# Copying the first attention's output tiles out of PSUM on another engine, and at another place in its program

## What is computed

```python
x = x + _L0_attn_ref(_layernorm(x), Mq, Mk, Mv)
x = x + _L0_ffn_ref(_layernorm(x), w_gate, w_up, w_down)   # blockwise FP4 rounding of x, weights and hidden values
x = x + _L1_attn_ref(_layernorm(x), w_qkv, ...)            # 16 heads of 16, layer norm of q and k
x = x + _L1_ffn_ref(_layernorm(x), W, b, R, A, B)          # top 2 of 8 low-rank experts
```

```python
scores = jnp.einsum('bhqk,bhck->bhqc', q, k).reshape(B * H, C, C)
att = jax.nn.softmax(scores / jnp.sqrt(jnp.float32(K)), axis=1)
out = jnp.einsum('bqhc,bhcd->bqhd', att.reshape(B, C, H, C), v)
```

## Time and profile before

| | us |
|---|---|
| median of 3 runs | 2735.5 (2731.2 to 2738.0) |
| the profiled execution, its own time | 2732.15 |
| its span, first to last instruction | 2730.4 |
| TensorE busy | 2515.6 (92%) |
| VectorE busy | 2032.0 (74%) |
| ScalarE busy | 1932.9 (71%) |
| GpSimd busy | 1211.5 (44%) |
| mean granted TensorE clock | 0.989 of full speed |

### The profile page before, as it was taken

How to read it: one execution, slowest core, us unless ns; L and a number is a source line. 1 busy time by engine, 2 the same in 40 slices (tenths; PEclk the granted TensorE clock), 3 DMA queues, 4 the chain that set the end, 5 groups by cost and what they waited for, 6 DMA issues and landing times.

```text
span 2730.4 us, 114318 instructions
## 1 busy us (share of the span) xinstructions
PE 2515.6 (92%) x50126; PEld 1391.3 (51%) x50126; DVE 2032.0 (74%) x4228; ACT 1932.9 (71%) x2767; POOL 1211.5 (44%) x1744
## 2 busy tenths in 40 slices
PE   6776877999999999999999999999999999999898
PEld 4445654345744566345654466445663457433434
DVE  6778866967888589866888589875888678875634
ACT  4552456886778767877778867787668777787685
POOL 4564466226743277125752167223772157411300
PEclk9988999999999999999999999999999999999999
DMA  5214332325423353324423343233532253232410
GB/s 133 47 37 82 60 67 75 67 42 96 112 54 82 60 120 79 70 51 85 109 72 77 50 98 92 63 66 59 122 93 53 51 99 91 61 70 41 92 37 25
DMA packets 458137, 200.60 MB, mean 73 GB/s; under 512 B 270110, under 2 KB 447622, under 8 KB 457614
## 3 DMA queue, kind: packets, MB, share of 16 engines
q1 hardware_dynamic: 455982, 192.15, 33.5%
q10 hardware_dynamic: 1632, 0.79, 0.2%
HBM read 46.48 MB, written 32.51 MB: 29 GB/s over the span
## 4 chain that ended last, share of the span: by engine, by line
PE 43%; DVE 22%; ACT 9%; DMA 8%; POOL 6%; issue 6%; SPq 4%; ACTq 0%; DVEq 0%; POOLq 0%
PE pR L765 16%; PE pV L1032 10%; ACT ub L1345 6%; DVE nmaxa L1648 6%; PE pS L989 6%; PE pS L765 5%; PE pV L890 3%; PE pR L775 2%; DMA xT<-ua 2%; DMA ua<-ua 2%; SPq L2655 1%; POOL ua L2182 1%; SPq L716 1%; DMA ua<-EA 1%; DMA xT<-xhb 1%
## 5 line engine op out<-in xcount | busy, mean ns | idle before, releaser
L1345 ACT ACTIVATE ub<-pS 128x1024 f32<-128x1024 f32 x1024 | 988.5, 1023 | 208.3 <-PE pS L989 198.9
L1648 DVE TENSOR_REDUCE nmaxa<-pS 128x1 f32<-128x1024 f32 x512 | 620.8, 1216 | 147.8 <-PE pS L765 145.2
L1281 ACT ACTIVATE ua<-pS,nmaxa 128x1024 f32<-128x1024 f32 x384 | 427.5, 1114 | 248.8 <-DVE nmaxa L1648 244.7
L765 PE MATMUL pS<-ua 128*32 128x512 f16 x8192 | 540.9, 384 | 59.9 <-ACT ua L1281 34.5
L1032 PE MATMUL pV<-ub,vaug 128*17 128x512 f32 x4096 | 536.0, 597 | 0.6 <-DVE ub L1826 0.2
L2182 POOL TENSOR_TENSOR ua<-ua,rz 128x256 f32<-128x256 f32 x512 | 329.7, 657 | 282.7 <-DVE rz L1657 274.7
L989 PE MATMUL pS<-ub 50*128 50x512 f16 x1920 | 312.0, 383 | 23.2 <-ACT ub L1345 18.5
L765 PEld LDWEIGHTS pS<-ua 128*32 128x32 f16 x8192 | 208.0, 97 | 222.5 <-ACT ua L1281 55.0
L765 PE MATMUL pR<-wgu,xT 128*32 128x352 f16 x6144 | 281.5, 316 | 22.9 <-DMA xT<-ua 11.5
L890 PE MATMUL pV<-ua 128*32 128x128 f32 x6144 | 240.4, 277 | 29.2 <-POOL ua L2182 26.6
L989 PEld LDWEIGHTS pS<-ub 50*128 50x128 f16 x1920 | 77.4, 93 | 348.8 <-ACT ub L1345 299.2
(11 more groups left out here) (274 smaller groups left out, 4096.4 us busy)
## 6 DMA issues: line engine op xcount, KB each, us to landing
ua<-ua SPq DMA_DIRECT2D x378, 128.0 KB, 2.8
ub<-scr SPq DMA_DIRECT2D x264, 64.0 KB, 2.6
scr<-ub SPq DMA_DIRECT2D x30, 512.0 KB, 4.1
x<-in_L_attn_x SPq DMA_DIRECT2D x32, 256.0 KB, 4.0
between<-x SPq DMA_DIRECT2D x28, 256.0 KB, 3.1
ub<-between SPq DMA_DIRECT2D x28, 256.0 KB, 3.6
out<-ub SPq DMA_DIRECT2D x28, 256.0 KB, 3.1
ub<-scr SPq DMA_DIRECT2D x192, 32.0 KB, 1.9
```

Of the source, the lines that this page charges most:

```text
L765: i = e.matmul(dst[j:j + 32], w[:, j:j + 32], m, start=start, stop=stop)
L1281: e.activation(EA[n % 4], pS[:, 1024 * (n % 2):1024 * (n % 2) + 1024], ACT.Exp, bias=nmaxa[:, n % 32:n % 32 + 1], accum_out=zz[:, n % 8:n ...
L1345: e.activation(EB[(2 * n + hp) % 4], pS[:, 1024 * hp:1024 * hp + 1024], ACT.Exp).then_inc(e1_in, 1)
L1648: e.tensor_reduce(nmaxa[:, n % 32:n % 32 + 1], pS[:, 1024 * (n % 2):1024 * (n % 2) + 1024], AXX, ALU.max, negate=True).then_inc(max0_in, 1)
```

## The change

In batches 2 to 7 the copy is taken out of VectorE's program and put into ScalarE's, as one instruction per output tile, at new places 11.4 + 8g (the last one 67.0). Since the exponentials stand at whole steps, place 11.4 is behind exponential 8g+11 and ahead of exponential 8g+12. The last product of the tile stands in TensorE's program at 10.8 + 8g. Batches 0 and 1 keep their places. TensorE's, GpSimd's and SyncE's programs stay as they are, and so do all waits; 48 instructions leave VectorE and 48 come to ScalarE.

```diff
-    ('ACT', 'outputs0'): (10.031, 18.823, 26.013, 34.45, 41.229, 50.468, 58.571, 76.219),
+    ('ACT', 'outputs0'): (11.4, 19.4, 27.4, 35.4, 43.4, 51.4, 59.4, 67.0),
+    ('ACT', 'outputs0', 0): (10.031, 18.823, 26.013, 34.45, 41.229, 50.468, 58.571, 76.219),
     ('ACT', 'outputs0', 1): (9.236, 18.295, 26.706, 34.378, 41.941, 51.483, 56.381, 66.317),
-    ('ACT', 'outputs0', 2): (),
...
-    ('DVE', 'outputs0'): (10.892, 12.014, 18.443, 21.518, 26.744, 28.254, 34.551, 36.466, 42.827, 44.855, 51.008, 55.442, 59.184, 63.996, 68.377,
-        70.128),
+    ('DVE', 'outputs0'): (12.014, 21.518, 28.254, 36.466, 44.855, 55.442, 63.996, 70.128),
...
             @timed("ACT")
             def outputs0(b):
-                for g in range(8 if b < 2 else 0):
+                for g in range(8):
                     yield
                     e.wait_ge(pv0_in, 64 * b + 8 * g + 8)
                     if g:
...
             @timed("DVE")
             def outputs0(b):
                 for g in range(8):
-                    yield
-                    if b > 1:
-                        e.wait_ge(pv0_in, 64 * b + 8 * g + 8)
-                        if g:
-                            full(("o0T", b, g - 1))
-                        e.tensor_copy(oTa[:, :], pV[:, 0:256]).then_inc(o0_in, 1)
                     yield
                     u = full(("o0T", b, g))
                     e.tensor_tensor(x[b % 2][:, g, :], x[b % 2][:, g, :], bank(u)[:, 0:256], ALU.add).then_inc(r_free[u.bank], 1)
```

## The result

The changed kernel takes 2789.7 us (median of 4 runs, 2787.3 to 2792.6) against 2734.8 us before: ratio 1.0197, interval 1.0179 to 1.0216, so 55 us slower. Forecast: 2780, range 2755 to 2810, slower with 0.90.

The account below looks back on a forecast made before the run. TensorE was taken as the bound, VectorE close behind. Waits of 9.5 us less 2.0 absorbed, times 6 batches, add 45 us; against the median 2780.5, rounded to 2780 us, range 2755 to 2810.

Parts of the forecast that it names:

- The bound and the mechanism: First attentions, batches 2 to 7: TensorE bounds; product 8g+8 waits for the copy behind exponential 8g+11, delaying everything after it.
- rival 1: First attentions: VectorE is the bound, waits are absorbed and 48 removed copies gain 15 us, giving 2720; chance 0.04.
- Terms 1 and 2: TensorE's waits at product 8g+8, tiles 0 to 6 (12.45 us), and at the second attention's first product (0.88): 13.3 us per batch.
- Term 3: VectorE, five of eight tiles: removing the copy brings maximum 8g+11 forward 0.32 us, 1.6 us per batch, leaving 11.7.
- the lower bound: If VectorE catches up while TensorE waits, tile 0's wait shrinks to 0.8 us; scaled, 5.5 us per batch.
- I take 9.5: The wait chosen per batch, 9.5 us, nearer the upper end because VectorE's queue won't empty at every tile.
- Term 4: TensorE's present idle time in the first attention, 6.4 us, absorbs 2.0 us per batch; the DMA wait moves along.
- The clock: TensorE's granted clock stays at full speed in these stretches, its busy time within a few us of 2516.
- The edits costed at nothing: ScalarE's 48 extra instructions (18 us), exponential 8g+12 up to 1.1 us later, and later residual adds on VectorE cost nothing.

Follow-up runs that it names:

- the kernel with tiles 4 and 5: Against the kernel before: in batches 2 to 7 ScalarE copies only tiles 4 and 5, at the change's late places; 2766.9 us, ratio 1.0118.
- VectorE's late copies: Against the kernel before: VectorE copies tiles 0 to 6 of batches 2 to 7 directly behind maximum 8g+12; 2829.3 us, ratio 1.0349.
- the filled kernel: The change plus 4 useless TensorE matmuls ahead of each wait for the copy of tiles 0 to 6, batches 2 to 7; 2783.4 us, again 2786.9 us.

## Why the prediction was right, point by point

**The bound and the mechanism** held. The loss follows the place of the copy on either engine, and it follows which tiles are moved and not how many. No run supports rival 1. The Trainium skill ("Perfetto Trace Analysis", Optimizing Scalar/DVE Operations) says that offloading work from a saturated VectorE to ScalarE may make sense; here 42 copies so moved were worth 7 us at most, and that only with the bank released in time. One reading was loose: the prediction put the new place two exponentials later than the data need. In batch 4 before the change, product 8g+7 ended ahead of exponential 8g+10 at tiles 1, 2, 3 and 6, where that holds, but during it at tiles 0, 4 and 5, where the place was one exponential too late.

**Terms 1 and 2.** The waits came to 70.1 us in the 48 places (66.1 at the products, 4.0 at the second attention, which the waits list puts down to "issue"), 11.7 per batch. The tiles' means over the six batches, in order, are 1.51, 1.24, 1.40, 1.21, 1.95, 2.69, 1.01 and 0.67, against 2.01, 1.02, 1.92, 1.27, 2.41, 2.64, 1.18 and 0.88 worked out from the earlier trace rows. Batch 4 did not stand for all at tile 1: the same subtraction in the trace before gives 1.02 to 1.72 there, 1.38 in the mean.

**Term 3 and the lower bound.** I took 9.5 us per batch between 5.5 and 11.7, and measured was the upper end. Where the copy had stood close before the maximum, the wait shrank (tile 0: from 2.01 to 1.55 in batch 4), but VectorE did not catch up further: in batch 4, maximum 8g+11 of tile 0 still starts 0.90 us behind its scores (1.23 before), nearer by the slot of the removed copy and no more. Tile 0 was also the wrong one to scale by. At tile 5, which waits longest, the maximum started 0.04 us behind its scores in both kernels, so nothing was there to catch up. The step that failed in size is "I take 9.5".

**Term 4.** Taken 2.0 us per batch, measured 70.1 - 48.8 = 21.3 us or 3.6 per batch. So the part of the loss that is idle time was (11.7 - 3.6) x 6 = 49 us, against 45 forecast: two errors of 2.2 and 1.6 us per batch, most of which cancel, and that is luck. The reading that failed is that the DMA wait moves along with the residual adds. Before, then after (both rows lie wholly behind 460 us):

```profile
PE pR L765 <- DMA xT<-ua: 14.5, 11, 3.5
```

```profile
PE pR L757 <- DMA xT<-ua: 5.5, 6, 1.5
```

It gave up 9.0 us, the largest part of the 21.3. Scaled values gave 5.8 us, another DMA (`ua<-ua`) 3.2 and the exponential in `EA` 3.3. Why the transposing DMAs kept their time while TensorE fell behind was not tested.

**The clock.** "The granted clock stays at full speed in these stretches" was wrong, and "TensorE's busy time stays within a few us of 2516": it rose to 2531, 8 us of it behind 460 us. These 8 us and the 4 by which 49 exceeds 45 lead from the forecast's 45 to the 57 by which the span grew; by the medians it is 55.

**The edits costed at nothing** cost nothing, by the run with ScalarE's extra copies. Their indirect effect is in the trace, though: in batch 4's stretch ScalarE waits 4.1 us in 5 places for product 8g+8 before exponential 8g+12, and no wait of TensorE shows it: those for exponentials sum to 1.1 us in the stretch, and to 1.3 before. Neither that later exponential nor the later residual adds were tested by themselves.

## What to carry to other kernels

When a copy out of PSUM frees the only bank, ask what stands ahead of it in the new engine's program and when the next writer of that bank is due; a place "behind the last product" in a table may be one long instruction too late. The duration of the copy and the load of the two engines decide little beside that: here 55 us by the place, at most 7 us by the engine. Find the earliest instruction of the copying engine behind which the data are surely ready, and put the copy directly there, ahead of other stages' work.

## What the runs showed of the hardware that was not expected

TensorE's granted clock, close to 1.0 behind 460 us before, fell to half for short times in the kernels with long waits. Three stretches of 7 us in the kernel after, each around a wait for `oTa` (tile 5 in batches 4 and 3, tile 1 in batch 2; the clock is the third figure from the end):

```profile
1412.00:1419.00 7.00, 4.29 (x120) 3.13 (x116) 5.08 (x7) 4.66 (x9) 4.70 (x4) 1.00 0.23 63
1089.00:1096.00 7.00, 5.42 (x112) 4.22 (x116) 3.46 (x4) 2.73 (x6) 3.50 (x4) 0.76 0.29 82
678.00:685.00 7.00, 4.87 (x82) 2.79 (x77) 1.94 (x3) 2.33 (x6) 4.80 (x9) 0.76 0.29 59
```

A mean of 0.76 over 7 us is half speed (1.2 instead of 2.4 GHz) for about half of it. In batch 4 the wait of 2.7 us at tile 5 left the clock up; in the second profile of the same program it fell there:

```profile
1409.00:1416.00 7.00, 4.30 (x88) 3.38 (x88) 3.85 (x4) 3.93 (x8) 4.69 (x4) 0.76 0.27 75
```

So the same wait costs more in one execution than in another. Behind 460 us there were 3 such drops before, 7 after (8 in its second profile), 11 in the kernel with tiles 4 and 5, 22 with VectorE's late copies, and at most 2 with the waits filled. (The one at the very end of each program is left out.) In the four profiles with long waits for `oTa` (the change twice, tiles 4 and 5, VectorE's late copies), 40 of the 68 such waits of 1.9 to 2.7 us have a drop that begins within 1.6 us of the wait's end, and none of the 70 shorter ones has. Of the change's 7 drops 5 are of this kind; the other two stand at waits for other engines that the kernel before has as well. The 19 drops that VectorE's late copies had more than the kernel before go with 31 us more of busy time, so each costs TensorE under 2 us. By this estimate the clock's part of the change is about 7 of the 55 us; filling the waits took 6 and 8 us off in the two comparisons. The Trainium skill ("TensorE: Matmul & The Clock Gate", HAM oscillation) tells of waits between groups of matmuls that bring the clock down, in a kernel whose matmuls wait 3 to 5 us for DMAs. The trace agrees in kind, and the waits that did it here are shorter, 1.9 to 2.7 us, once per tile. That the filled kernel's gain is the clock's alone is not shown: the useless matmuls also turn the rotation of the ring banks.
